# Six tiles of gathered rows fetched row by row by SyncE, one memset between early gathers, and 124 gathers ahead of the first scatter

## What is computed

```
row, col = src, dst
deg      = number of edges whose src is a node
norm     = rsqrt(deg[row]) * rsqrt(deg[col])      # 0 where a degree is 0
h        = relu(layernorm(x))
msg[e]   = alpha[type] * norm * sum_b comps[type, b] * (h[col[e]] @ bases[b])      # 4 bases of 128x128
out      = x + segment_sum(msg, row)
```

## Time and profile before

| | us |
|---|---|
| median of 3 runs | 722.61 |
| profiled execution, its own time | 723.03 |
| its span in the trace | 721.2 |
| VectorE busy | 593.3 (82%) |
| TensorE busy | 562.8 (78%) |
| GpSimd busy | 562.7 (78%) |
| ScalarE busy | 364.7 (51%) |

### The profile page before, as it was taken

The page is one execution under the profiler, slowest core; times in us unless marked ns, Lnnn a source line. Parts: engine busy times, 40 slices in busy tenths (PEclk is TensorE's granted clock), DMA queues, the critical chain, the costliest instruction groups (busy, mean ns, idle before and its releaser), DMA issues.

```text
span 721.2 us, 13608 instructions
## 1 busy us (share of the span) xinstructions
PE 562.8 (78%) x3922; PEld 399.7 (55%) x3922; DVE 593.3 (82%) x2624; ACT 364.7 (51%) x1494; POOL 562.7 (78%) x532
## 2 busy tenths in 40 slices
PE   4999996666667888567799879977888888889940
PEld 3766665444455665345566656655666566655620
DVE  7999999468768798656999999989999989997820
ACT  0345354545444888335556545664555565546620
POOL 3888888777778878878788878877888878776885
PEclk9999999789897999877999999999999999999975
DMA  8899999989984546344544554454545545444332
GB/s 278 274 344 322 348 324 325 344 294 315 312 297 68 97 85 121 52 77 65 110 69 88 91 107 84 86 96 91 85 96 96 99 80 98 80 60 85 33 34 25
DMA packets 56573, 108.88 MB, mean 151 GB/s; under 512 B 9339, under 2 KB 48264, under 8 KB 55684
## 3 DMA queue, kind: packets, MB, share of 16 engines
q0 software_dynamic: 34496, 25.72, 26.9%
q1 hardware_dynamic: 4688, 50.95, 19.1%
q10 hardware_dynamic: 17316, 31.36, 14.2%
HBM read 94.89 MB, written 64.61 MB: 221 GB/s over the span
## 4 chain that ended last, share of the span: by engine, by line
DVE 45%; PE 21%; issue 10%; DMA 9%; ACT 7%; POOL 7%; ACTq 1%; SPq 0%; POOLq 0%; DVEq 0%
DVE masked L477 9%; PE pst L737 8%; DVE part_sum L514 8%; PE pst L756 8%; DVE turned_hot L471 6%; DVE rows L454 6%; POOL out_dram L389 6%; DVE same L533 4%; DVE rows L455 4%; DVE rows L514 4%; DMA out_dram<-rows,scatter_idx 3%; DMA edge_row<-edge_rows 2%; ACT part_sum L646 2%; PE pst L764 2%; PE pst L766 2%
## 5 line engine op out<-in xcount | busy, mean ns | idle before, releaser
L389 POOL DMA_INDIRECT out_dram<-rows,scatter_idx x196 | 313.2, 1598 | 78.3 <-issue 46.4
L368 POOL DMA_INDIRECT rows<-in_x_dram,dst_i x196 | 226.4, 1155 | 68.9 <-issue 27.7
L737 PE MATMUL pst<-table_bits,turned_hot 128*128 128x198 f16 x1568 | 176.1, 260 | 72.1 <-DVE masked L477 53.5
L756 PE MATMUL pst<-bases_sb,h_turned 128*128 128x512 f32 x392 | 212.8, 626 | 0.0
L737 PEld LDWEIGHTS pst<-table_bits,turned_hot 128*128 128x128 f16 x1568 | 141.9, 102 | 100.1 <-issue 50.2
L514 DVE SCALAR_TENSOR_TENSOR part_sum<-pst,coef,part_sum 128x128 f32<-128x128 f32 x392 | 115.6, 344 | 77.3 <-ACT part_sum L646 65.3
L646 ACT ACTIVATE part_sum<-pst,coef 128x128 f32<-128x128 f32 x196 | 71.1, 363 | 167.1 <-PE pst L756 129.1
L764 PEld LDWEIGHTS pst<-rows,same 128*128 128x128 f32 x392 | 72.3, 196 | 149.0 <-issue 121.6
L477 DVE SCALAR_TENSOR_TENSOR masked<-iota_h,lo,pst 128x198 f32<-128x198 f16 x392 | 141.8, 416 | 10.9 <-PE pst L737 7.9
L764 PE MATMUL pst<-rows,same 128*128 128x128 f32 x392 | 81.0, 289 | 43.1 <-ACT rows L653 38.3
L591 ACT ACTIVATE scratch<-rows 128x128 f32<-128x128 f32 x196 | 57.9, 299 | 73.1 <-DMA rows<-in_x_dram,dst_i 72.7
(11 more groups left out here) (72 smaller groups left out, 438.5 us busy)
## 6 DMA issues: line engine op xcount, KB each, us to landing
out_dram<-in_x_dram SPq DMA_DIRECT2D x46, 1000.0 KB
src_row<-src_rows ACTq DMA_DIRECT2D x25, 512.0 KB
edge_row<-edge_rows ACTq DMA_DIRECT2D x44, 256.0 KB
out_dram<-in_x_dram ACTq DMA_DIRECT2D x4, 1000.0 KB
rows<-in_x_dram,dst_i POOLq DMA_INDIRECT x196
out_dram<-rows,scatter_idx POOLq DMA_INDIRECT x196
rows<-edge_rows ACTq DMA_DIRECT2D x10, 175.0 KB
edge_row<-edge_rows SPq DMA_DIRECT2D x5, 256.0 KB
```

Source lines behind the costliest of these rows:

```text
L368: pool.indirect_dma_start(row(t), None, x, bass.IndirectOffsetOnAxis(ap=dst_i[:, t:t + 1], axis=0)) \
L389: pool.indirect_dma_start(out, bass.IndirectOffsetOnAxis(ap=scatter_idx[:, t:t + 1], axis=0), row(t), None, compute_op=ALU.add) \
L737: last = pe.matmul(pst[:, LOOK + t % 2, k * LO:(k + 1) * LO], turned_hot[:, g % 2, c, k * W + j * P:k * W + (j + 1) * P], table[:, c * LO: ...
L756: pe.matmul(pst[:, PRODUCT + t % 4, :], h_turned[:, g % 2, j, :], bases_sb[:].rearrange("d b f -> d (b f)"), start=True, stop=True).then_i ...
```

## The change

FIRST_GATHERS goes from 120 to 124, and the second memset between the gathers behind the histogram goes. Tiles 186 to 191 (half of group 46, the whole of group 47) are no longer gathered by GpSimd, which now has 190 gathers; SyncE fetches their 768 rows with one DMA of 512 bytes each. It first loads the 768 indices into SBUF. Then, for four rows at a time, it loads four indices into registers and issues four DMAs. Four rows go behind each copy from piece 6 on (44 pieces, 176 rows), and the other 592 behind the last copy. The early tables move down from the last tiles to the tiles ahead of 186. `stats_until` stops at 46 groups, and from step 40 on it allows all 49, so that ScalarE's groups 46, 47 and 48 all fall to step 40.

```
-    HIST_GATHERS, FIRST_GATHERS = 56, 120
+    HIST_GATHERS, FIRST_GATHERS = 56, 124
+    ROW_TILES = range(186, 192)
+    ROW_STEP = 40
+    ROW_LOAD = 4
+    POOL_TILES = [t for t in range(TILES) if t not in ROW_TILES]
     def gathers_until(t):
-        return min(TILES, FIRST_GATHERS + t // 2)
+        return min(len(POOL_TILES), FIRST_GATHERS + t // 2)
     def stats_until(step):
-        return min(STATS_BEFORE + 2 * (step + 1), gathers_until(sums_until(step - 1)) // GROUP)
+        if step >= ROW_STEP:
+            return GROUPS
+        return min(STATS_BEFORE + 2 * (step + 1), gathers_until(sums_until(step - 1)) // GROUP, ROW_TILES[0] // GROUP)
...
-        EARLY_TILE = TILES - -(-early // D)
+        EARLY_TILE = ROW_TILES[0] - -(-early // D)
...
+        row_idx = sb("row_idx", [len(ROW_TILES), P], I32)
...
+            sp.dma_start(row_idx[:], dst[ROW_TILES[0] * P:(ROW_TILES[-1] + 1) * P].rearrange("(t p) -> t p", p=P)) \
+                .then_inc(row_idx_loaded, 16)
+            def fetch_rows(a, b):
+                for r in range(a, b, ROW_LOAD):
+                    q, p = divmod(r, P)
+                    t = ROW_TILES[q]
+                    _, nodes = nc.values_load_multi_w_load_instructions(
+                        row_idx[q:q + 1, p:p + ROW_LOAD], engines=[mybir.EngineType.SP], min_val=0, max_val=N - 1,
...
+                    for i, node in enumerate(nodes):
+                        sp.dma_start(row(t)[p + i:p + i + 1, :], x[bass.ds(node, 1), :]) \
+                            .then_inc(row_fetched[t // GROUP - ROW_TILES[0] // GROUP], 16)
+            fetched = 0
             for i in range(FIRST_COPIES, COPIES):
                 copy(sp, i)
+                if i == FIRST_COPIES + COPY_RING:
+                    sp.wait_ge(row_idx_loaded, 16)
+                if i >= FIRST_COPIES + COPY_RING:
+                    fetch_rows(fetched, fetched + ROW_LOAD)
+                    fetched += ROW_LOAD
+            fetch_rows(fetched, len(ROW_TILES) * P)
...
-            def pace(t):
+            def pace(n):
...
-                    for _ in range(2):
-                        beats[0] += 1
-                        pool.memset(beat[:], 0.0).then_inc(beat_ended, 1)
-                        pool.wait_ge(beat_ended, beats[0])
+                    beats[0] += 1
+                    pool.memset(beat[:], 0.0).then_inc(beat_ended, 1)
+                    pool.wait_ge(beat_ended, beats[0])
-            def gather(t):
+            def gather(n):
+                t = POOL_TILES[n]
...
             def row_sums(g):
-                act.wait_ge(row_gathered[g], 16 * GROUP)
+                fetched = sum(t in ROW_TILES for t in range(g * GROUP, (g + 1) * GROUP))
+                if fetched < GROUP:
+                    act.wait_ge(row_gathered[g], 16 * (GROUP - fetched))
+                if fetched > 0:
+                    act.wait_ge(row_fetched[g - ROW_TILES[0] // GROUP], 16 * P * fetched)
```

More of the change, by code:

```diff
@@ L80, in build @@
     SUM_STEP, SUM_RATE = 3, 5
-    HIST_GATHERS, FIRST_GATHERS = 56, 120
+    HIST_GATHERS, FIRST_GATHERS = 56, 124
[3 more added lines that the diff above has]
+    POOL_TILES = [t for t in range(TILES) if t not in ROW_TILES]
+    assert ROW_TILES[-1] < E // P
     def gathers_until(t):
-        return min(TILES, FIRST_GATHERS + t // 2)
+        return min(len(POOL_TILES), FIRST_GATHERS + t // 2)
     def sums_until(step):
@@ L146, in build @@
         type_hot = part(TW, BF16).rearrange("p (b e) -> p b e", b=2)
-        assert at[0] <= TILES * D
+        assert at[0] <= ROW_TILES[0] * D
         def row(t):
@@ L228, in build @@
         beat_ended = sem("beat_ended")
+        row_idx_loaded = sem("row_idx_loaded")
+        row_fetched = [sem(f"row_fetched{g}") for g in sorted({t // GROUP for t in ROW_TILES})]
         type_row_loaded = [sem(f"type_row_loaded{b}") for b in range(TYPE_RING)]
@@ L326, in _ @@
                 load_src_row(sp, i)
+            sp.dma_start(row_idx[:], dst[ROW_TILES[0] * P:(ROW_TILES[-1] + 1) * P].rearrange("(t p) -> t p", p=P)) \
[6 more added lines that the diff above has]
+                        row_idx[q:q + 1, p:p + ROW_LOAD], engines=[mybir.EngineType.SP], min_val=0, max_val=N - 1,
+                        skip_runtime_bounds_check_because="an edge's end is a node, and the DMA checks its address")
+                    for i, node in enumerate(nodes):
+                        sp.dma_start(row(t)[p + i:p + i + 1, :], x[bass.ds(node, 1), :]) \
+                            .then_inc(row_fetched[t // GROUP - ROW_TILES[0] // GROUP], 16)
+            fetched = 0
             for i in range(FIRST_COPIES, COPIES):
                 copy(sp, i)
+                if i == FIRST_COPIES + COPY_RING:
[4 more added lines that the diff above has]
+            fetch_rows(fetched, len(ROW_TILES) * P)
             sp.wait_ge(spare_filled, 16)
@@ L350, in _ @@
             beats = [0]
-            def pace(t):
-                if 0 < t < HIST_GATHERS:
-                    pool.wait_ge(hot_used, t * TILES // HIST_GATHERS)
-                elif HIST_GATHERS <= t < FIRST_GATHERS:
-                    for _ in range(2):
-                        beats[0] += 1
-                        pool.memset(beat[:], 0.0).then_inc(beat_ended, 1)
-                        pool.wait_ge(beat_ended, beats[0])
-            def gather(t):
+            def pace(n):
+                if 0 < n < HIST_GATHERS:
+                    pool.wait_ge(hot_used, n * TILES // HIST_GATHERS)
+                elif HIST_GATHERS <= n < FIRST_GATHERS:
+                    beats[0] += 1
[3 more added lines that the diff above has]
+                t = POOL_TILES[n]
                 g = t // GROUP
-                pace(t)
+                pace(n)
                 if t == EARLY_TILE:
@@ L372, in _ @@
             pool.wait_ge(idx_ready, 1)
-            for t in range(FIRST_GATHERS):
-                gather(t)
+            for n in range(FIRST_GATHERS):
+                gather(n)
             gathered = FIRST_GATHERS
```

## The result

The changed kernel took 799.01 us (median of four runs, 796.99 to 801.4), the kernel before 722.63 (four runs) beside it: a ratio of 1.106, 95% interval 1.103 to 1.109. The profiled execution took 801.4 us, its span 799.5. The forecast, 721.9 in a range to 736, was wrong by 77 us. The same kernel, run an hour later on the chip numbered 10 (eight runs), took 723.57 (ratio 0.998, interval 0.995 to 1.002), which is close to the forecast. The record doesn't give the number of the chip that the first figure comes from. So the result has two halves: what the change does by itself, and something that it sets off in some sets of runs and not in others.

A forecast was written before the change was run, and what follows sets the result against it. Bound by stage: GpSimd's gathers before the first scatter, GpSimd and ScalarE in step with VectorE almost equal, GpSimd alone after step 40. 723.03 - 1.2 - 0 - 3.5 + 4.0 = 722.3 profiled, 721.9 median; range 709 to 736.

The forecast's parts named there:

- 1, the first scatter: Up to the first scatter, waiting for GpSimd's gathers and the copies: 1.2 us saved, bounds 6.3 saved to 20 lost.
- A: Rival: SyncE's rows come late for ScalarE's wait in step 40, from 0.71 us a row; 752 us at 0.76; chance 0.17.
- D: Rival: GpSimd is the bound throughout, so ten gathers less save 13.3 us, giving 708.1 us; chance 0.12.
- B: Rival: one DMA engine carries SyncE's rows and the copies end 3 to 15 us later; 729 us at 8; chance 0.15.
- 2, SyncE's rows: SyncE's row fetches: 0.55 us a row, the last near 536 us, in time for step 40, so nothing lost.
- 3, steps to 31: First scatter to step 31, GpSimd and ScalarE coupled: no change of its own, bounds -2 to +2 us.
- 4, steps 31 to 40: Steps 31 to 40, where ScalarE no longer waits for gathers: 3.5 us saved, bounds 0 and 6.
- 5, step 40: Step 40, where three of ScalarE's groups fall: at least 13.1 us long, 4.0 us lost.
- C: Rival: ScalarE's burst of 8.8 us in step 40 is hidden, so the 4.0 us loss goes: 717.9 us; chance 0.18.
- 6: The rest: 36 scatters from tile 160 on, 72 us as before, so no change.

The follow-up runs named there:

- d3: The changed kernel run again unaltered, on chip 10: 723.6 us, ratio 0.998 to the kernel before.
- a3: The kernel before with one memset instead of two behind the histogram and 124 early gathers, no rows by SyncE: 723.1 us on chip 12, ratio 0.999.
- c2: a3 with three more semaphores that nothing uses, on chip 2: 775.2 us, ratio 1.071 to the kernel before.
- d1: a3 run again unaltered, on chip 10: 719.7 us, ratio 0.993 to the kernel before.
- b1: The changed kernel with its one memset between early gathers lengthened from 40 to 380 columns, on chip 6: 737.7 us, ratio 1.018.
- d4: The changed kernel with the second memset put back, on chip 10: 734.2 us, ratio 1.013 to the kernel before.
- b2: The changed kernel with SyncE fetching rows at fixed addresses, no indices loaded to registers, on chip 6: 793.8 us, ratio 1.096.
- b4: The changed kernel with SyncE fetching only group 47's four tiles, all behind the last copy, on chip 6: 791.3 us, ratio 1.092.

## Why the prediction was wrong

By its own steps, with d3 for what the change does undisturbed (profiled execution 720.5, forecast 722.3):

**1, the first scatter: this is the step that failed.** It let the first scatter wait for two things, GpSimd's gathers and the copies: saved 1.2 us, bounds +6.3 and -20 (the -20 doesn't follow from the step's own 46 us either). In the result it lost 69.0. The gathers themselves came as worked out (mean 1.42 us for 1.47, the last at 212.5 for 211.8). The step left out a third wait, for the summed rows of tile 0, at the end of the look-ups and the first steps on VectorE, TensorE and ScalarE: GpSimd stood 73.67 us before the first scatter until ScalarE's L693 gave them. What I took as given was that this work, which runs beside the gathers, doesn't depend on their spacing. The mechanism that the profile shows is none of A to D: VectorE starts on finished look-ups 5 to 27 us after TensorE has ended them, while the gathers last. No row of before has it, at a spacing of 1.66 us.

Undisturbed the step was too cautious: the first scatter came at 213.15, 5.0 sooner. GpSimd was done at 208.5 and the copies ready 0.3 ahead of the scatter, at 212.85 (before about 213.5), so eight more gathers and 176 rows delayed them by nothing that can be seen; of the step's terms for the copies, 3.1 us, none came. B's loss of 3 to 15 us didn't come either. From 300 to 400 us of d3 queue q1 moves 350 packets for 176 rows, two a row, as the sum had it.

**2, SyncE's rows: right.** Predicted 0.55 us a row and the last at 536; measured (546.9 - 206.2) / 595 = 0.573 and 547, long before step 40 at 625.6. An issue is 225 ns at the median, with 37 and 29 for the address, and a load of four indices 558. The Trainium skill gives a floor of about 600 ns for such a load ("DMA: Bandwidth & Descriptors", section "Latency and other measured facts"). The trace goes below it, 558 at the median and 460 at the shortest behind the copies; during the copies, with full queues, a load takes 745. Rival A falls. In the disturbed execution it was 357.4 / 595 = 0.601 us a row, still in time.

**3, steps to 31: right.** 201.58 and 201.39 us for 201.3. The early part of the stretch, first scatter to step 12, took 1.0 us more in d3 (116.09 for 115.07). Two long waits for gathers stay there, 1.53 and 11.37 us.

**4, steps 31 to 40: right in sign, mis-sized.** Saved 1.3 us (94.74 for 96.0) and 1.6 in the other trace, not 3.5. ScalarE's waits for gathers were down to one, of 0.7 us in d3 (4.5 us in four before), but VectorE is busy 88.55 of the 94.74 us, and that leaves little to gain.

**5, step 40: right.** 13.64 us in both traces, at least 13.1 predicted; lost 4.9 for the 4.0, of which step 41 gave back 1.4 (8.37 for 9.8). C falls: the burst isn't swallowed.

**6: right.** 70.1 us from tile 160 to the last scatter for 71.0. D falls with it: ten gathers less were worth 1.3 us.

So the balance of the change by itself is -5.0 + 1.0 + 0.3 - 1.3 + 4.9 - 1.4 for what stands above and -1.1 behind step 41, -2.6 us for the -0.7 forecast. The two traces are of different sets, and the medians within one set can't be told apart (0.998, 0.995 to 1.002). That 723.6 came out beside the 721.9 forecast is in part luck: step 1 was 3.8 us too cautious, and steps 4 and 5 were 2.2 and 0.9 too hopeful. What the forecast lacked was any chance for an interaction that the trace of before can't show; its range ended at 736 as the sum of priced terms.

No version is better than the kernel before wherever it runs. a3 was the fastest on chips 10 and 4 (0.993 and 0.987, the second from two runs), equal on 12, and its twin c2 is 7% slower on chip 2; rows by SyncE add nothing to it (d3 against d1: 723.6 and 719.7). I would keep the two memsets.

## What to carry to other kernels

A pause that seems idle may be of use: where a wait or a memset only spaces the issues of one engine, ask what the other engines hand to each other meanwhile, and leave a margin when it is shortened. List every wait of an instruction that is to come sooner, the ones that end early today too: the first scatter had three, and I priced two. When an experiment is to show which part of a change does harm, put the changed kernel itself in each set: without it a chip that doesn't show the harm looks like a part that doesn't cause it. In a trace, a releaser "remote" in a program on one core, with a partner that finished microseconds ago, marks a late hand-off and not work to be made shorter. Count the items on both sides before saying how late it is: with two places in a ring, the result that is picked is not the last one made.

## What the runs showed of the hardware

With one indirect gather of 128 rows every 1.37 us (mean 1.42), GpSimd can bring the rest of the core close to a halt in some sets of runs. In the result VectorE starts on TensorE's finished look-ups 5 to 27 us after their end, waiting 3.6 to 14.8 us each time, in place of waits of at most 0.9; TensorE starts 0.15 us after VectorE's pick; and register instructions of SyncE go from 37 to as much as 724 ns. VectorE's waits end with the last of these gathers, SyncE's slow instructions don't quite (up to 746 ns until 615 us). At 1.63 us and above it was not seen for longer than one wait of VectorE (b1, 4.4 us, ended at 116.8), and that one began while b1's gathers still ran unpaced, 1.3 to 1.7 us apart; SyncE's register instructions reach 381 ns in b1, and 43 in d3 and d4 on chip 10.

Where between 1.43 and 1.63 us it begins, why the sets differ, and through what the signals and instructions are held up, stays open: no kernel between these spacings ran, no chip was visited twice, and nobody can choose the chip. That the spacing does it rests on b1 against b2 to b4 in one set and on the coincidence of begin and end; that something beside the kernel decides is shown by one kernel at 799 and at 723.6 us.
